# Hyperbolic attention stage: head-by-head storage, two chunks per ScalarE instruction, other rings

## What is computed

```python
q_h, k_h, v_h = exp_map(q), exp_map(k), exp_map(v)       # tanh of the norm, per head
arg    = max(1 + 2*c*|q_h - k_h|^2 / ((1 - c|q_h|^2)(1 - c|k_h|^2)), 1 + EPS)
dist   = arccosh(arg) / sqrt(c)                           # [2048 queries, 2048 keys] per head
w      = softmax(-beta * dist - bias)                     # over the keys
out    = log_map(exp_map(w @ log_map(v_h)))
y      = concat(out) @ W_o.T
```

## Time and profile before

| | |
|---|---|
| median of three runs | 7286.41 us |
| profiled execution, time | 7294.11 us |
| its span | 7292.3 us |
| PE busy in the span | 4547.1 us (62%) |
| DVE busy | 4717.3 us (65%) |
| ACT busy | 4687.7 us (64%) |
| POOL busy | 1329.5 us (18%) |
| mean granted TensorE clock | 0.762 |
| packets of the sums' queue (q0) | 536.90 MB, 36.6% of 16 engines |
| packets of SyncE's queue (q1) | 90.74 MB, 7.1% |

### The profile page before, as it was taken

How to read it: one execution, slowest core, us unless ns; L and a number is a source line. 1 busy time by engine, 2 the same in 40 slices (tenths; PEclk the granted TensorE clock), 3 DMA queues, 4 the chain that set the end, 5 groups by cost and what they waited for, 6 DMA issues and landing times. The chain is left out here.

```text
span 7292.3 us, 78431 instructions
## 1 busy us (share of the span) xinstructions
PE 4547.1 (62%) x23556; PEld 2300.8 (32%) x23556; DVE 4717.3 (65%) x6664; ACT 4687.7 (64%) x4434; POOL 1329.5 (18%) x1152
## 2 busy tenths in 40 slices
PE   7999999899999974343444434445344454445456
PEld 5666666666666662000000000002100010001004
DVE  5555555555555554776776767774767787768684
ACT  4544555455445542677787777886488888888893
POOL 0000000000000000332333323231233333333320
PEclk9999999999999986566666656666566666666666
DMA  1000000000000002777776777875468686878681
GB/s 32 6 6 6 9 6 6 5 6 6 7 6 9 2 3 58 126 145 131 137 136 124 150 135 131 150 145 122 104 132 165 140 159 133 165 139 159 133 174 58
DMA packets 330626, 631.71 MB, mean 87 GB/s; under 512 B 167814, under 2 KB 263752, under 8 KB 264264
## 3 DMA queue, kind: packets, MB, share of 16 engines
q0 software_dynamic: 73728, 536.90, 36.6%
q1 hardware_dynamic: 256584, 90.74, 7.1%
HBM read 69.50 MB, written 21.23 MB: 12 GB/s over the span
## 5 line engine op out<-in xcount | busy, mean ns | idle before, releaser
L1436 PE MATMUL psum<-b_qT,b_kT 126*128 126x512 bf16 x2048 | 894.4, 538 | 1855.4 <-DVE b_tiles L1195 1852.3
L1195 DVE SCALAR_TENSOR_TENSOR b_tiles<-b_ra_rep,b_cap,psum 128x1024 f32<-128x1024 f32 x1024 | 1261.1, 1271 | 1063.7 <-DMA b_tiles<-b_tiles 535.9
L1436 PEld LDWEIGHTS psum<-b_qT,b_kT 126*128 126x128 bf16 x2048 | 140.6, 109 | 2771.4 <-DVE b_tiles L1195 2715.7
L1329 ACT ACTIVATE b_tiles<-b_tiles 128x2048 f32<-128x2048 f32 x320 | 598.3, 1904 | 539.4 <-DVE b_tiles L907 449.1
L567 DVE CUSTOM_DVE_ANT_0 a_srow<-psum,a_bias 128x1024 f32<-128x1024 f32 (+7 forms) x768 | 679.2, 909 | 146.7 <-PE psum L703 74.1
L1202 DVE TENSOR_SCALAR b_tiles<-b_tiles 128x2048 f32<-128x2048 f32 x512 | 752.3, 1469 | 5.5
L638 ACT ACTIVATE a_srow<-a_srow,a_nmax 128x640 f32<-128x640 f32 (+15 forms) x512 | 615.8, 1203 | 121.2 <-DVE a_nmax L573 90.7
L1339 ACT ACTIVATE b_tiles<-b_tiles,b_sc 128x2048 f32<-128x2048 f32 x320 | 659.3, 2079 | 0.0
L1448 PE MATMUL psum<-b_tiles,b_v_aug 128*32 128x512 f32 x2560 | 548.8, 947 | 132.2 <-ACT b_tiles L1339 131.9
L1334 ACT ACTIVATE b_tiles<-b_tiles 128x2048 f32<-128x2048 f32 x320 | 599.8, 1898 | 0.9
L725 PE MATMUL psum<-ident,a_srow 128*128 128x128 f32 x4352 | 577.7, 277 | 16.7 <-DVE a_pT L484 11.5
(11 more groups left out here) (218 smaller groups left out, 7310.2 us busy)
## 6 DMA issues: line engine op xcount, KB each, us to landing
b_tiles<-b_tiles POOLq DMA_DIRECT2D x320, 1024.0 KB, 14.9
X<-b_tiles POOLq DMA_DIRECT2D x192, 1024.0 KB, 16.1
b_ra_rep<-ra_scratch SPq DMA_DIRECT2D x32, 1024.0 KB, 27.5
a_wqk<-in_wqk_dram SPq DMA_DIRECT2D x64, 128.0 KB, 2.8
x_scratch<-X SPq DMA_DIRECT2D x8, 1024.0 KB, 10.9
kv_scratch<-b_tiles SPq DMA_DIRECT2D x4, 2048.0 KB, 9.1
X<-x_scratch SPq DMA_DIRECT2D x8, 1024.0 KB, 10.6
X<-in_x_dram SPq DMA_DIRECT2D x4, 1024.0 KB, 9.5
```

The source lines that it names most:

```text
L1195: nc.vector.scalar_tensor_tensor(out=a[:, s * HALF:(s + 1) * HALF], in0=ra_rep[:, j, s * HALF:(s + 1) * HALF], scalar=cap[:, j, k:k + 1], ...
L1329: nc.scalar.activation(y, y, ACT.Sqrt, bias=-1.0).then_inc(S["root_done"], 1)
L1436: last = nc.tensor.matmul(half_ps(s)[:, i * BANK:(i + 1) * BANK], kT[:, j, k * P:(k + 1) * P], qT[:, j, cs], start=True, stop=True)
```

## The change

- `tok` is laid out by head: (head, token tile, 16 values) instead of (token tile, head, 16 values), and so are the per-head factors, `kv_scratch` and `ra_scratch`. The k and v of a head are then one run of 1 KB per partition, and `ra_rep` is loaded as one run of 8 KB per partition. k and v land in `k_raw` and `v_raw`, and GpSimd copies them on. The final scaling writes into `out_tok` in the order of tokens.
- `a` gets a ring of seven slots, `y` one of ten, numbered through the chunks of a batch.
- ScalarE's root, log and exp each take two chunks (4096 columns) in one instruction; a pair's log is followed at once by its exp.
- `prep` becomes `prepare` in three parts, placed behind the groups of sums 1, 2 and 3 of a head, for the head two ahead; `take_v` copies v.
- Loops over batches and head pairs are written out, 32 heads one after another on each engine.

```diff
-A_SLOTS = [6, 7, 8, 9, 14, 2] * 2 + [6, 7, 8, 9, 14] * 4
-Y_SLOTS = [10, 11, 12, 13, 15, 16, 17, 18, 3, 4, 5] * 2 + [10, 11, 12, 13, 15, 16, 17, 18, 3, 4]
+A_SLOTS = [6, 7, 8, 9, 14, 2, 5]
+Y_SLOTS = [10, 11, 12, 13, 15, 16, 17, 18, 3, 4]
+A_BACK, Y_BACK = len(A_SLOTS), len(Y_SLOTS)
...
-        tok = tiles[:, 0:6, :].rearrange("p s n -> p (s n)").rearrange("p (a t d) -> p a t d", a=3, d=D)
+        tok = tiles[:, 0:6, :].rearrange("p s n -> p (s n)").rearrange("p (a h t d) -> p a h t d", a=3, h=HB, d=DB)
+        out_tok = tiles[:, 2:4, :].rearrange("p s n -> p (s n)").rearrange("p (t d) -> p t d", d=D)
...
+        k_raw = sb("k_raw", [P, TB * DB])
+        v_raw = sb("v_raw", [P, TB * DB])
...
+        def a_slot(h, k):
+            return tiles[:, A_SLOTS[(h * NCHK + k) % A_BACK], :]
+        def y_slot(h, k, n=1):
+            s = Y_SLOTS[(h * NCHK + k) % Y_BACK]
+            slots = tiles[:, s:s + n, :] if s < 15 else x_ring[:, s - 15:s - 15 + n, :]
+            return slots.rearrange("p s n -> p (s n)")
...
-        def prep(eng, engine, b, h, j, alone):
...
+        def prepare(eng, engine, b, h, part, alone=False):
             g = b * HB + h
-            n = [0]
+            n = [(0, 6, 10)[part]]
...
+            if part == 0:
                 sync()
-                for i, places in enumerate((Q_PARTS, K_PARTS)):
-                    step(engine.tensor_tensor(aug[:, i, :, :], aug[:, i, :, :], stack[:, i, :, places[part][0], :],
-                                              ALU.subtract))
+                step(engine.tensor_copy(aug[:, 0, :, 0:DB], rows(0)))
+                step(engine.tensor_copy(aug[:, 0, :, DB:DB + 1], of(NS_Q)))
+                step(engine.memset(aug[:, 0, :, DB + 1:AUG], 1.0))
+                step(engine.tensor_copy(aug[:, 1, :, DB:DB + 1], of(E_K)))
+                step(engine.tensor_copy(aug[:, 1, :, DB + 1:AUG], of(EN_K)))
+                if alone:
+                    k = rows(1)
+                else:
+                    eng.wait_ge(S["k_loaded"], (b * (HB - 1) + h) * 16)
+                    k = k_raw[:, :].rearrange("p (t d) -> p t d", d=DB)
+                step(engine.tensor_copy(aug[:, 1, :, 0:DB], k))
                 sync()
-            sync()
-            assert n[0] == PREP, n[0]
-            eng.sem_inc(S["stack_done"], 1)
+            elif part == 1:
+                eng.wait_ge(S["grpT_done"], g * 4)
+                split("h")
+                sync()
+                rest("h")
+                sync()
+            else:
+                if h >= 2:
+                    eng.wait_ge(S["scores_read"], (g - 1) * 2 * NCHK)
+                step(engine.tensor_copy(cap[:, h % 2, :].unsqueeze(2), of(CAP_K)))
+                split("m")
+                sync()
+                rest("m")
+                sync()
+                split("l")
+                sync()
+                eng.sem_inc(S["stack_done"], 1)
+            assert n[0] == (6, 10, 17)[part], n[0]
+        def take_v(eng, engine, b, h, alone=False):
+            g = b * HB + h
             if alone:
-                engine.tensor_copy(v_aug[:, j, :, 0:DB], toks(2)).then_inc(S["v_ready"], 1)
-                return
-            for i in range(NCHK // BATCHED):
-                if i:
-                    squares(eng, engine, g - 1, i, 1 - j)
-                sums(eng, engine, g - 1, i, 1 - j)
+                v = tok[:, 2, bass.ds(h, 1), :, :].rearrange("p a t d -> p (a t) d")
+            else:
+                eng.wait_ge(S["av_done"], av((g - 1) * NCHK))
+                eng.wait_ge(S["v_loaded"], (b * (HB - 1) + h) * 16)
+                v = v_raw[:, :].rearrange("p (t d) -> p t d", d=DB)
+            engine.tensor_copy(v_aug[:, h % 2, :, 0:DB], v).then_inc(S["v_ready"], 1)
...
+                kv = kv_scratch[bass.ds(b, 1)].rearrange("b a p (h n) -> p (b a) h n", h=HB)
...
+                    return kv[:, i, bass.ds(h, 1), :].rearrange("p a n -> p (a n)")
...
+                    sp.wait_ge(S["pool_step"], (b * HB + h - 1) * PREP + 6)
+                    sp.dma_start(k_raw[:, :], of_head(0, h)).then_inc(S["k_loaded"], 16)
+                def load_v(h):
+                    sp.wait_ge(S["v_ready"], b * HB + h)
+                    sp.dma_start(v_raw[:, :], of_head(1, h)).then_inc(S["v_loaded"], 16)
+                def load_ra(h):
                     g = b * HB + h
+                    sp.wait_ge(S["scores_read"], (g - 1 if h >= 2 else g - h) * 2 * NCHK)
+                    src = ra_scratch[bass.ds(b, 1)].rearrange("a (h t) k -> (a h) (t k)", h=HB)[bass.ds(h, 1)]
+                    sp.dma_start(ra_rep[:, h % 2, :], src.to_broadcast([P, SEQ])).then_inc(S[f"ra_loaded{h % 2}"], 16)
+                load_ra(0)
+                for h in range(1, HB):
+                    load_k(h)
+                    load_v(h)
+                    load_ra(h)
...
-                prep(pool, nc.gpsimd, b, 1, 1, False)
-                with pool.Fori(0, HB // 2 - 1) as i:
-                    prep(pool, nc.gpsimd, b, i * 2 + 2, 0, False)
-                    prep(pool, nc.gpsimd, b, i * 2 + 3, 1, False)
-                for n in range(NCHK // BATCHED):
-                    squares(pool, nc.gpsimd, b * HB + HB - 1, n, 1)
-                    sums(pool, nc.gpsimd, b * HB + HB - 1, n, 1)
+                for part in range(3):
+                    prepare(pool, nc.gpsimd, b, 1, part)
+                squares(pool, nc.gpsimd, b, 0, 0)
+                last = NCHK // BATCHED - 1
+                for h in range(HB):
+                    for n in range(last + 1):
+                        sums(pool, nc.gpsimd, b, h, n)
+                        if n < last:
+                            squares(pool, nc.gpsimd, b, h, n + 1)
+                        elif h + 1 < HB:
+                            squares(pool, nc.gpsimd, b, h + 1, 0)
+                        if n == 2 and h + 1 < HB:
+                            take_v(pool, nc.gpsimd, b, h + 1)
+                        if n > 0 and h + 2 < HB:
+                            prepare(pool, nc.gpsimd, b, h + 2, n - 1)
...
-                    if back < 8 and (k >= back or not first):
-                        dve.wait_ge(*summed(g, k - back))
...
+                    if h or k >= A_BACK:
+                        dve.wait_ge(*summed(g, k - A_BACK))
...
-                nc.vector.tensor_tensor(o3, o3, ons[:, 1, :].unsqueeze(2).to_broadcast([P, TB * HB, DB]), ALU.mult
-                                        ).then_inc(S["o_scaled"], 1)
+                nc.vector.tensor_tensor(out_tok.rearrange("p t (h d) -> p h t d", d=DB), tok[:, 0, :, :, :],
+                                        ons[:, 1, :].rearrange("p (h t) -> p h t", h=HB).unsqueeze(3).to_broadcast(
+                                            [P, HB, TB, DB]), ALU.mult).then_inc(S["o_scaled"], 1)
...
-                        nc.scalar.activation(tok[:, :, t, :], ps.rearrange("p (a n) -> p a n", a=3), ACT.Copy
-                                             ).then_inc(S["tok_copied"], 1)
+                        nc.scalar.activation(tok[:, :, :, t, :].rearrange("p a h d -> p (a h) d"),
+                                             ps.rearrange("p (n d) -> p n d", d=DB), ACT.Copy).then_inc(S["tok_copied"], 1)
...
+                def root(h, k):
+                    g = b * HB + h
+                    for i in range(k, k + 2):
+                        act.wait_ge(S["sq_" + SQUARES[i]], squared(g, i) + 1)
+                    y = y_slot(h, k, 2)
                     nc.scalar.activation(y, y, ACT.Sqrt, bias=-1.0).then_inc(S["root_done"], 1)
+                def log(h, k):
+                    g = b * HB + h
+                    for i in range(k, k + 2):
+                        act.wait_ge(*summed(g, i))
+                    y = y_slot(h, k, 2)
                     nc.scalar.activation(y, y, ACT.Ln).then_inc(S["ln_done"], 1)
+                def weight(h, k):
+                    g = b * HB + h
+                    act.wait_ge(S["ln_done"], pairs_to(g, k))
+                    y = y_slot(h, k, 2)
                     nc.scalar.activation(y, y, ACT.Exp, bias=col(SHIFT), scale=col(NEG_S)).then_inc(S["w_done"], 1)
-                def weights(g, n, j):
+                def roots(n):
+                    for k in range(n * BATCHED, (n + 1) * BATCHED, 2):
+                        root(k // NCHK, k % NCHK)
+                def weights(n):
                     nc.scalar.preload_act_table_set("natural_log_exp_and_others")
-                    ks = range(n * BATCHED, (n + 1) * BATCHED)
-                    for k in ks:
-                        log(g, k, j)
-                        if k > ks[0]:
-                            weight(g, k - 1, j)
-                    weight(g, ks[-1], j)
+                    for k in range(n * BATCHED, (n + 1) * BATCHED, 2):
+                        log(k // NCHK, k % NCHK)
+                        weight(k // NCHK, k % NCHK)
+                NB = HB * NCHK // BATCHED
                 act.wait_ge(S["x_saved"], (b + 1) * 64)
```

(18 more changed lines are left out.)

239 lines of the change are left out of this document (72 added, 167 removed).

## The result

The kernel after takes 6438.07 us (median of 4 runs, 6434.41 to 6439.15), the kernel before 7287.01 on the same chip: a ratio of 0.8834 (0.8819 to 0.885), 849 us less. The forecast was 6490 with a range from 6405 to 6750. The profiled execution has a span of 6437.1 us, against 7292.3.

A forecast was written before the change was run, and what follows sets the result against it. Sums held up by the slow load and the preparation starved ScalarE. Each batch's run becomes 84 + 62 x 25.1 = 1640 us, saving 457 and 307; with first loads' 24 and 13, 801 together, hence 6490, range 6405 to 6750.

The forecast's parts named there:

- The chain: Hyperbolic stage: a sum (DMA add of `a` into `y`) lands late, VectorE lacks a slot, squares come late, ScalarE starves.
- ScalarE's instructions: Two-chunk instructions take 3.61 us (root, log) and 3.79 (exp), making a round of four chunks 24.5 us, 0.7 shorter.
- The start of a run: A batch's run until the second group of roots is done takes 52 us, where it took 60.
- The loop through all engines: From ScalarE's exp through TensorE and VectorE to a later root: 23.6 us, slack 0.9; slowed, 25.1 us per round.
- Room for a late sum: Against the loop a sum has some 7 us of room, covering the new load (5 us) and the preparation (2 us).
- The first rival: The ra_rep load stays slow: 434 us more, about 6920; chance 0.14, shared with a load cured only in part.
- the second rival: The loop binds harder, 2 to 3 us more per round: 6830, or 6690 at its near end; chance 0.15.
- The load: ra_rep's broadcast load in 8 KB runs takes 5 us (ends 2.5 and 28.9); first loads save 24 and 13 us.
- The rule on pitch: For ra_rep, whose blocks lay 8 KB apart: rows a large power of two apart copy slowly, so one row cures it.
- Preparation in parts: GpSimd's preparation cut in three, same work of about 13 us per head, delays the next sums by 0 to 2 us.
- Rings: `a` goes from five or six slots to seven, `y` from ten or eleven to ten; no price of their own.
- Code: Written-out heads fetch about 45 code pieces per batch; as third rival, 1340 us more, 7830; chance 0.05 with other causes.

The follow-up runs named there:

- experiment 1: Kernel after with ra_scratch stored by token tile again, so ra_rep loads as 512-byte blocks 8 KB apart: 6748.28 us.
- experiment 5: Kernel after with GpSimd's preparation in one piece again, ahead of the next head's first sums: 6506.82 us.
- 8: Kernel after with the ring of `a` cut from seven slots to five: 6892.18 us.
- experiment 3: Kernel before with the load alone changed (ra_scratch stored by head, ra_rep read as 128 runs of 8 KB): 6802.85 us.
- experiments 10 to 12: Kernel after with the next head's transposes spread over two rounds (6411.44 us), with TensorE's product 11 chunks behind the scores instead of 10 (6411.93), and with both (6411.79).
- experiment 6: Kernel after with one chunk per ScalarE instruction instead of two for root, log and exp: 6485.13 us.
- experiment 4: Kernel after with k and v read in 2048 runs of 64 bytes again: 6437.29 us.
- experiment 9: Kernel after with the preparation in one piece and one chunk per ScalarE instruction, both: 6484.74 us.
- the lag of 11: Kernel after with TensorE's product of a chunk's weights with v put 11 chunks behind its scores instead of 10: 6411.93 us.

## Why the prediction was right

The mechanism held step by step, and the forecast was 52 us too long of 849.

- *The chain.* Late sum, no slot, late squares, starved ScalarE: shown by experiments 1, 5 and 8, which bring late sums or missing slots back, and 3, which takes one cause away.
- *ScalarE's instructions.* Predicted 3.61 and 3.79 us and a round of 24.5; measured 3.61, 3.80 and 24.54. The estimate that I had worked out from the fixed cost of 0.19 us in the Trainium skill ("VectorE: DVE Perf Modes", the section on the TRN2 errata), a round 0.4 us shorter than mine, is 24.1; the round of the trace doesn't agree. The fixed cost does: the roots' 1.904 and 3.613 us at 2048 and 4096 columns leave 0.195. The 0.29 that I had called the trace's fixed part belongs to the exponentials of attention a alone. What the estimate left out is the overlap: of two roots the second starts 3.53 us behind the first, which lasts 3.62, so that an instruction less saves some 0.1 us (0.65 for the six of a round).
- *The start of a run.* Predicted 52 us until the second group of roots is done; measured 2891.88 to 2943.5, 51.6.
- *The loop through all engines: the term that was mis-sized.* I set 25.1 us per round. The run of batch 0 gives (1618.3 - 51.6 - 32.2) / 62 = 24.75. I had found a slack of 0.9 us and taken it as used up in most rounds by slower clamps and by copies. It is used up in one of four, the one where transposes and their copies lie in the loop; experiments 10 to 12 take that wait away, and experiment 6 hides it. 62 x 0.35 is 22 us per batch, 43 of the 52 missed.
- *Room for a late sum.* Predicted some 7 us; a sum that is 9.6 us late makes VectorE wait 3.2 and a round of ScalarE 2.2 longer, so it is 6.4 at the one and 7.4 at the other (experiment 5). The cover held. The first rival's price was too high all the same (6920, where the slow load takes 6748): I had charged the load's whole time less the room, 21 and 10 us a head, where it costs 14.1 and 5.4 (experiment 1). What I left out is the lead of the load over the sums: it is issued at 3008.18 there and the sums at 3013.5, so 27.7 us of load hold them for 22, and less 7.4 of room that is an estimate of 15.
- *The near end of the second rival.* I put it at 6690. 2 us more on a round of 25.1 gives 84 + 62 x 27.1 = 1764, twice 124 more than 1640, so 6738; the range took that in, but only just.
- *The load.* Predicted 5 us, between 2.5 and 28.9; measured 6.7, covered in mid-head. The first loads gave 24.7 and 13.6 us (24 and 13).
- *The rule on pitch* (the Trainium skill, "DMA: Bandwidth & Descriptors", the section on latency and other measured facts: copies are slow when the partitions' rows lie a large power of two apart; the pitches measured there are 512 KiB to 8 MiB). At 8 KB, far below them, the runs show a slow load too: 26.2 us, against 8.3 at 576 bytes with equal runs. That the power of two is what matters at 8 KB no run shows, and channel aliasing stays an inference; the many partitions reading one row are no trouble (6.7 us).
- *k and v.* Predicted nothing, measured nothing (experiment 4).
- *Preparation in parts.* The delay of 0 to 2 us came true (2.2). What I did not see is that the cut only matters beside the pairs (experiment 9): I costed both by themselves.
- *Rings.* I gave them no price, only the loop that follows. They and the written-out heads hold the largest part after the load, 318 us; how much of it is theirs and how much that of the heads was not taken apart. The 454 us for two slots point to the rings but are no share of the 318: with five slots and all the rest of the change the kernel takes 6892 us, more than the kernel of experiment 3 with five or six slots and the load alone (6803).
- *Code.* About 45 pieces of instruction code per batch predicted; the DMA view of 2892 to 4510 has 29, and no gap on ScalarE is put down to issue:

```profile
q8 instruction: 29, 0.48, 0.1%
```

The sum by windows: 479 + 328 + 24.7 + 13.6 = 845 us, where the steps gave 801. The other 10 us of the span's 855 lie between the batches: two gaps on VectorE of 6.7 and 3.6 us that the profile of before puts down to issue aren't there after. I had not counted them, and their cause wasn't tested.

## What to carry to other kernels

When a stage has one engine that would be full, count its round, and then the loop that must close within it; the time is the longer of the two in each round, and a copy or a transpose moved into another round can be worth half as much as larger instructions (26 us here, against 47). Price a ring's slot by what it covers in every round, not only where the worst delay is, and price edits that share one slack together: here a cut worth 69 us beside larger instructions is worth nothing without them. An engine that stops waiting hasn't become the faster part: look whether its instructions have grown by what the waits have shrunk.

## What the runs showed of the hardware

- A 1 MB broadcast to 128 partitions in runs of 512 bytes lands in 26.2 us with the runs 8 KB apart, and in 8.3 us with them 576 bytes apart; in runs of 8 KB in 6.7 us. While the slow one runs, the sums on another queue come to a stand as well (44 GB/s in all, and in 10 us no packet of theirs).
- A clamp of 128x2048 takes 1.2 us alone. With the lag of 11 single ones beside GpSimd's square of 3.6 us take up to 4.6, and the mean over the kernel is 1.84 us. In the kernel after the square has all but ended when a clamp starts (1.28 us then, in mid-run): VectorE's waits of 2.7 us had kept it out of GpSimd's way.
- A square root of 4096 columns takes 3.61 us and one of 2048 takes 1.90, which leaves a fixed part of 0.195 to each; instructions in a row overlap by some 0.1 (3.62 us long, 3.53 apart).
